# A second norm's inverse deviations inside an attention loop: Newton rounds on VectorE, or a first guess from ScalarE's tables

## What is computed

```
x = x + tanh(g1) * attention(layernorm(x), ctx, ctx)     16 heads of 8 channels
x = x + tanh(g2) * ffn(layernorm(x))
layernorm(x) = (x - mean) / sqrt(var + 1e-5)             over the 128 channels of a token
ffn(x) = mean over 2 shared experts + top 2 of 8 routed experts, 128 -> 512 -> 128, exact gelu
```

## Time and profile before

| | |
|---|---|
| median of 3 runs | 459.96 us (459.46 to 460.46) |
| the profiled execution | 462.34 us, its span 460.2 us |
| TensorE's mean granted clock | 0.968 |
| busy: DVE, PE | 387.0 us (84%), 386.7 us (84%) |
| busy: ACT, POOL | 339.0 us (74%), 310.6 us (67%) |

### The profile page before, as it was taken

One profiled execution on the slowest core, in us unless ns is written; L12 is line 12 of the kernel. 1 busy time (PEld: TensorE's weight loads), 2 busy tenths in 40 slices (PEclk: granted clock), 3 DMA queues, 4 the chain that ended last, 5 costly groups with the idle time before them and its releaser, 6 DMA issues.

```text
span 460.2 us, 14622 instructions
## 1 busy us (share of the span) xinstructions
PE 386.7 (84%) x5155; PEld 317.5 (69%) x5155; DVE 387.0 (84%) x950; ACT 339.0 (74%) x674; POOL 310.6 (67%) x431
## 2 busy tenths in 40 slices
PE   0566889996999899988779899998999999999910
PEld 0344767775888788776537676776899999999910
DVE  7797568977867977899788999887699999999986
ACT  0635678785888788878677987775788888888844
POOL 6252222898799999978777647775077777777740
PEclk9999899999999999999899999999899999999965
DMA  8967784354344244474121111112223333346129
GB/s 197 318 189 218 184 182 117 86 133 95 91 95 112 65 121 98 107 255 176 37 61 54 42 37 47 48 48 65 69 69 110 96 94 93 92 135 185 57 75 291
DMA packets 71685, 53.42 MB, mean 116 GB/s; under 512 B 7209, under 2 KB 63476, under 8 KB 71616
## 3 DMA queue, kind: packets, MB, share of 16 engines
q1 hardware_dynamic: 64896, 43.15, 35.5%
q0 software_dynamic: 4544, 8.44, 5.6%
q10 hardware_dynamic: 2176, 0.91, 0.8%
HBM read 29.51 MB, written 24.33 MB: 117 GB/s over the span
## 4 chain that ended last, share of the span: by engine, by line
POOL 30%; DVE 20%; issue 16%; PE 12%; DMA 11%; ACT 4%; SPq 3%; POOLq 0%; ACTq 0%; DVEq 0%
POOL yd L650 14%; DMA scr<-QKS 5%; POOL xs L628 3%; DVE HH L1532 3%; PE pAtt L1090 2%; POOL QKS L548 2%; DVE t_MX L1257 2%; POOL t_STG L558 2%; DMA t_K<-scr 2%; POOL t_W2l L562 2%; PE pS L1027 2%; DMA t_STG<-in_W 1%; POOL t_XF L572 1%; PE pE L1027 1%; PE pAtt L928 1%
## 5 line engine op out<-in xcount | busy, mean ns | idle before, releaser
L650 POOL DMA_INDIRECT yd<-Y,XR x78 | 87.4, 1121 | 38.4 <-issue 23.5
L1257 DVE TENSOR_REDUCE t_MX<-pS 128x4 f32<-128x512 f32 x128 | 86.7, 682 | 23.8 <-PE pS L889 21.6
L748 ACT ACTIVATE PT<-pE,t_mbias,t_scl 128x512 f32<-128x512 f32 x128 | 96.8, 787 | 3.7 <-PE pE L889 3.7
L628 POOL DMA_INDIRECT xs<-t_STG,t_pos x64 | 66.5, 1039 | 26.8 <-issue 13.4
L1562 DVE SCALAR_TENSOR_TENSOR HR<-GG,t_sc,HR 128x512 f16<-128x512 f32 x78 | 58.6, 751 | 2.8
L1144 PE MATMUL pAtt<-t_W2h,HR 128*128 x624 | 59.1, 219 | 0.7 <-DVE HR L1562 0.7
L889 PE MATMUL pS<-t_K,t_Q 128*128 128x128 f16 x512 | 50.9, 224 | 8.5 <-DVE t_MX L1257 5.4
L1144 PE MATMUL pAtt<-t_W2l,HR 128*128 x312 | 54.4, 219 | 0.0
L889 PE MATMUL pE<-t_Q,t_K 128*128 128x128 f16 x512 | 50.5, 222 | 2.6 <-DMA t_Q<-MPl 1.6
L828 ACT ACTIVATE GG<-pS,t_b1T,t_inv 128x256 f32<-128x256 f32 x78 | 39.8, 560 | 17.0 <-PE pS L1132 16.5
L1090 PE MATMUL pAtt<-t_W2h,HH 128*128 128x128 f16 x512 | 47.8, 222 | 4.3 <-DVE HH L1532 4.3
(11 more groups left out here) (280 smaller groups left out, 1041.8 us busy)
## 6 DMA issues: line engine op xcount, KB each, us to landing
xs<-t_padrow SPq DMA_DIRECT2D x10, 516.0 KB, 5.2
XR<-xs SPq DMA_DIRECT2D x39, 129.0 KB, 2.3
scr<-QKS SPq DMA_DIRECT2D x16, 256.0 KB, 2.4
t_Q<-scr SPq DMA_DIRECT2D x16, 256.0 KB
t_K<-scr SPq DMA_DIRECT2D x32, 128.0 KB
t_STG<-in_W SPq DMA_DIRECT2D x7, 512.0 KB, 6.8
YY<-yd SPq DMA_DIRECT2D x14, 256.0 KB, 4.6
t_X<-in_x SPq DMA_DIRECT2D x4, 512.0 KB, 7.3
```

The source lines that it names most:

```text
L628: g.indirect_dma_start(k.xs, bass.IndirectOffsetOnAxis(ap=pos[:, n:n + 1], axis=0), k.PAY[:, n, :], None).then_inc(h.di[q], 16)
L650: g.indirect_dma_start(k.yd, bass.IndirectOffsetOnAxis(ap=XR[u][:, q, D:ROW], axis=0), Y[u][:, q, :], None, bounds_check=2 * T - 1, oob_is ...
L748: act.activation(PT[:, m % NPT], pE[g % 2][:], ACT.Exp, bias=k.mbias[:, bt:bt + 1], scale=k.scl[:, bt:bt + 1]).then_inc(s.exp, 1)
L1257: v.tensor_reduce(out=MX[:, n // G % 2, n % G // 4, m % 2, m // 2::2], in_=pS[n % 2][:], axis=AX_X, op=ALU.max).then_inc(s.max, 1)
```

## The change

For the turns 8, 12, 16 and 18 the first guess comes from ACT: DVE adds epsilon in step 0 and raises a semaphore; ACT computes in its step 2 the logarithm, then `exp(-0.5 * ln(var + eps))` into `k.rstd`, and raises a second one; DVE waits for it in step 4, does one Newton round, two instructions of it in step 4 and the third in step 5, and `k.nmr` behind it. In turn 18 the generator is now called once per step as in the others. The pairs 14 and 15, after the loop, are computed as before. Three semaphores of the prologue are joined with others to make room for the three new ones; their instructions stay where they were.

```diff
+    SEEDED = sorted(t for t in RSTD if t < END)
...
+            def seed_deviations(t):
+                first, pairs = RSTD[t]
+                cols = slice(2 * first, 2 * (first + pairs))
+                act.wait_ge(l.var, SEEDED.index(t) + 1)
+                act.activation(tmpn[:, cols], tmpv[:, cols], ACT.Ln).then_inc(l.ln, 1)
+                act.wait_ge(l.ln, SEEDED.index(t) + 1)
+                act.activation(k.rstd[:, cols], tmpn[:, cols], ACT.Exp, scale=-0.5).then_inc(l.seed, 1)
...
+                    if g == 2 and t in SEEDED:
+                        seed_deviations(t)
...
+            def seeded_deviations(t):
+                first, pairs = RSTD[t]
+                cols = slice(2 * first, 2 * (first + pairs))
+                out, x, y = k.rstd[:, cols], tmpv[:, cols], tmpn[:, cols]
+                link(v.memset(tmpn[:, cols], 0.0))
+                link(v.tensor_scalar(x, k.mv[:, cols, 1], EPS, None, ALU.add))
+                settle(v, l.var)
+                for _ in range(4):
+                    yield
+                v.wait_ge(l.seed, SEEDED.index(t) + 1)
+                link(v.scalar_tensor_tensor(out=y, in0=out, scalar=-0.5, in1=out, op0=ALU.mult, op1=ALU.mult))
+                link(v.tensor_tensor(y, y, x, ALU.mult))
+                yield
+                link(v.scalar_tensor_tensor(out=out, in0=y, scalar=1.5, in1=out, op0=ALU.add, op1=ALU.mult))
+                v.scalar_tensor_tensor(out=k.nmr[:, cols], in0=k.mv[:, cols, 0], scalar=-1.0, in1=out, op0=ALU.mult, op1=ALU.mult).then_inc(l.rstd, 1)
+                yield
...
-                rstd = inverse_deviations(*RSTD[t]) if t in RSTD else iter(())
+                rstd = seeded_deviations(t) if t in RSTD else iter(())
...
                     next(rstd, None)
-                    if t == END - 2:
-                        next(rstd, None)
-                        next(rstd, None)
```

More of the change, by code:

```diff
@@ L312, in layer @@
     names = ("xn T XT qk qk32 hi lo ST S max mp nmT t2 exp pv ev tk at bt cp op x "
-             "st vp vev dv bias bvr any gb scl wm wk wb ws wh wl mb mr md ma qs st1 rs z zz sq zk")
+             "st vp vev dv bias bvr any gb scl wm wk wb ws wh wl mb mr qs st1 rs z sq zk")
     s = Parts(**{n: sem("a_" + n) for n in names.split()})
@@ L318, in layer @@
     N_W, N_RD, N_M = 16 * 3, 16 * 4, 16 * 2
-    l = Parts(**{n: sem("l_" + n) for n in "rstd xf pay T XT G gate idx route count slots".split()})
+    l = Parts(**{n: sem("l_" + n) for n in "rstd xf pay T XT G gate idx route count slots var ln seed".split()})
     h = Parts(**{n: sem("s_" + n) for n in "up gelu hi hia lo dn x exp wt".split()})
@@ L476, in body @@
                     if t == 2:
-                        sp.wait_ge(s.z, 1)
+                        sp.wait_ge(s.z, NB - 1)
                     wait(sp, s.ST, G * (t - NB + 1))
@@ L677, in values_in @@
                 if t == 2:
-                    act.wait_ge(s.z, 1)
+                    act.wait_ge(s.z, NB - 1)
                 wait(act, s.pv, G * (t - NB + 1))
@@ L729, in _ @@
                 act.activation(k.Q[u][:].rearrange("p a b -> p (a b)").bitcast(F32).rearrange("p (n d) -> p n d", d=P), eights,
-                               ACT.Copy, scale=0.0).then_inc(s.zz, 1)
-            act.wait_ge(s.zz, NB - 2)
+                               ACT.Copy, scale=0.0).then_inc(s.z, 1)
+            act.wait_ge(s.z, NB - 2)
             for u in range(2, NB):
@@ L876, in _ @@
             pe.transpose(pA[0][:, 1, 0:B], k.maskf[:], k.identf[0:B, 0:B]).then_inc(s.mr, 1)
-            pe.wait_ge(s.md, 1)
+            pe.wait_ge(s.mb, 2)
             pe.matmul(pA[1][:, 0, 0:5], k.ones[0:5, :], k.mxd[:], start=True, stop=True)
-            pe.matmul(pA[1][:, 1, 0:B], k.ones[:], k.maskT[:], start=True, stop=True).then_inc(s.ma, 1)
+            pe.matmul(pA[1][:, 1, 0:B], k.ones[:], k.maskT[:], start=True, stop=True).then_inc(s.mr, 1)
             pe.wait_ge(k.s_rest, k.rest_in)
@@ L1173, in _ @@
             link(v.tensor_reduce(out=k.mxc[:], in_=pA[0][0:5, 0, :], axis=AX_X, op=ALU.max))
-            v.tensor_scalar(k.mxd[:], k.identf[0:5, 0:5], k.mxc[:], None, ALU.mult).then_inc(s.md, 1)
-            v.wait_ge(s.ma, 1)
+            v.tensor_scalar(k.mxd[:], k.identf[0:5, 0:5], k.mxc[:], None, ALU.mult).then_inc(s.mb, 1)
+            v.wait_ge(s.mr, 2)
             v.tensor_scalar(k.anyb[:], pA[1][:, 1, 0:B], 1.0, None, ALU.min)
```

## The result

The changed kernel is slower: 465.11 us median of 12 runs (462.39 to 466.88), beside 460.44 us (458.12 to 463.92) for the kernel before on the same chip. The ratio is 1.0101, with an interval of 1.0077 to 1.0125. The forecast of 455.5 us was wrong in its sign, and the time lies outside the range.

What follows compares the result with a forecast made beforehand. POOL was taken to set the pace in turns 8 to 15, DVE in turns 16 to 18. Terms 1.3 + 1.0 + 1.9 + 0.3 = 4.5 us took the median from 459.96 to 455.5 us, range 454.0 to 457.2, chance 0.62.

Steps and rivals of the forecast that it cites:

- The step that failed: ACT's first logarithm, in turn 8, brings the only added table load, 1.28 us, covered by ACT's wait of 2.24 us.
- Rival 3: Each of four seeds loads tables twice, 3.1 us on ACT: 463 us; chance 0.10, shared with any other slower way.
- Turn 12's overrun: Two loads in turn 12 exceed ACT's holes; the loss is mostly taken back by POOL's slower pace. No size given.
- Turn 8: The second Newton round leaves DVE, so nmr and POOL's payload 0 come 1.3 us earlier; bounds 0 and 2.8.
- ACT's part: Two small activations per seeded turn, 0.5 us together, plus one load, covered by ACT's waits behind step 3.
- Turn 16: PE's plain scores no longer wait 0.81 us for DVE and come earlier: 1.0 us, lower bound 0.
- Turn 18 with the clock: DVE's block leaves, closing PE's 2.09 us hole: 1.9 us (0 to 2.1); PE's clock may not fall: 0.3 (0 to 0.7).
- Payload 12, the tie: Turn 18's later nmr makes payload 12 ready at 223.3 to 223.8, against PE's transpose_rows at 224.0.
- granted clock at 1.00 through 226: Sign of being right: with PE's turn 18 wait of 2.09 us gone, its clock stays full, instead of 0.50 from 224.
- The sum: Gains in turns 8, 16 and 18 plus the clock, 1.3 + 1.0 + 1.9 + 0.3 = 4.5 us, giving median 455.5.

Runs made afterwards that it cites:

- pair in turn 12: Kernel with one set, with a table load put back before the logarithm and one before the exponential in turn 12 alone: 455.88 us, ratio 0.9922.
- pair in turn 18: Kernel with one set, with the two table loads put back around the logarithm in turn 18 alone: 457.50 us, ratio 0.9935.
- one load in turn 8: Changed kernel with one load of the joint Exp and Ln set right before turn 8's logarithm, no other added load: 452.42 us, again 453.24 us.
- only turn 18 spread: Kernel before, with turn 18's three Newton rounds spread one stage per step over steps 0 to 5, no guess from ACT: 458.52 us, ratio 0.9971.
- kernel with one set: Changed kernel with the set holding both Exp and Ln loaded once at the layer's start, no loads in the seeded turns: 454.85 us, again 454.48 us.
- loads alone: Kernel before with only two table loads added at step 2 of turns 8, 12, 16 and 18: 462.0 us, ratio 1.0066.
- pair in turn 8: Kernel with one set, with the two table loads put back around the logarithm in turn 8 alone: 452.94 us, ratio 0.9854.
- pairs in 8 and 12: Kernel with one set, with the two table loads put back around the logarithm in both turns 8 and 12: 456.93 us, ratio 0.9926.

## Why the prediction was wrong, point by point

**The step that failed** is the sentence "Ln was not used before, so a table load comes with the first one: 1.28 us". It put the whole of the loads at one, from the silent assumption that one set stays loaded for both functions. Eight came. With the one load that the step assumed, the kernel gives 452.4 and 453.2 us, a gain; with eight, 465.1. What spoke for one load was a set that holds both functions. The Trainium skill, "ScalarE: Activation LUTs", section "Table sets: the hidden batching unit", says that a logarithm followed by an exponential takes one load, as there is a set with both. The runs agree with the half of it that such a set exists and serves both: the load at 106.19 above. They disagree with the count for code that names no set: there, each guess loaded twice.

**Rival 3 was the right one, at the wrong price.** It named two loads per seed, 3.1 us on ACT (2.93 measured), and gave 463 us at a chance of 0.10. Three parts of the price were too small. "Turn 12's overrun" was "mostly taken back by POOL's slower pace": it was not, the pair there costs 2.4 to 2.9 us up to the Gelu load. PE stood 2.54 us, and ACT's next queries and keys came late to POOL (with the pair in turn 12 alone):

```profile
161.81 0.61 POOL L547 CAST QKS<-QK 128x512 f16<-128x512 f32 x1 [1.56 <-ACT QK L667]
```

In the changed kernel POOL waited 1.19 us for payload 4 and 1.31 us there. The second part is turn 18, where PE was to come "about 0.7 later than before": with the pair in turn 18 alone, the Gelu load came 1.9 us later than before, counted from payload 8 (24.39 less 22.45). And the clock was left out: over 104 to 232 us the granted clock of the changed kernel was 0.95 on average, against 1.00 and 0.99 in the two executions with one load in turn 8. How much time that is was not separated.

**Turn 8** (forecast 1.3 us). POOL's wait before payload 0 fell to 1.54 us in the changed kernel, and to 0.64 and 0.33 in the two executions with one load in turn 8. But that wait is a poor measure: it was 2.81 us in the kernel before and 1.54 in the one with only turn 18 spread, whose turn 8 is the same code. There the second round, from which the 1.3 was read, took 0.7 us instead of 1.33: two of its instructions took 0.17 and 0.25 us where the profile of before had 0.54 each. So the 1.3 was read from one execution and does not repeat. By these waits the term lies between 0.9 and 2.5 and stays no sharper.

**ACT's part, other than the loads**, was right. Two activations of 0.21 us, and a cover of ACT's wait in turn 8 that shrinks "to under 0.6": 0.57 and 0.17 with one load there. That 0.57 is so close to 2.24 less (1.28 + 0.5) is luck, as the same wait without a load in the turn was 1.03 and 1.56.

**Turn 16** (forecast 1.0). Without the added loads payload 7 to payload 8 takes 8.08 us instead of 9.48: 1.4 us.

**Turn 18 with the clock** (forecast 1.9 + 0.3). Payload 8 to the Gelu load falls from 22.45 to 20.29 us: 2.2 us. The hole of 2.09 us is gone and the clock stays at 1.00 up to the Gelu load. The experiment with the block spread shows that the reason given, the block's place, carries 1.7 of the 2.2 up to that mark, but 1.0 of 2.2 up to PE's first matmul of the shared experts.

**Payload 12, the tie.** With one set, PE waits 0.74 us for it in turn 19; with the eight loads, POOL has it at 224.98 after a wait of 4.94 us. The 0.74 us alone are the small loss that a tie allows. But the forecast's sign "granted clock at 1.00 through 226" held only in part, and right behind this wait. Of the four executions with one load, two keep 1.00 there and two do not. PE's wait, then two windows of the first execution of the kernel with one set, then the same two windows of its second (columns as above):

```profile
220.21 0.40 PE L980 MATMUL pMix<-t_ident,t_STG 128*128 128x128 f16 x4 [0.74 <-POOL t_STG L578]
```

```profile
220.00:222.00 2.00, 1.51 (x11) 1.06 (x12) 1.13 (x5) 1.58 (x5) 1.69 (x5) 1.00 0.00 0
222.00:224.00 2.00, 2.00 (x21) 1.39 (x20) 0.88 (x4) 1.03 (x3) 1.71 (x3) 1.00 0.00 0
```

```profile
220.00:222.00 2.00, 1.72 (x10) 0.93 (x8) 0.76 (x4) 1.18 (x5) 1.85 (x5) 0.70 0.00 0
222.00:224.00 2.00, 2.00 (x12) 1.16 (x12) 0.83 (x3) 0.27 (x1) 1.40 (x3) 0.50 0.00 0
```

**The sum.** Turn 8's term aside, the rows give 1.4 + 2.2 = 3.6 us, where the forecast had 3.2. With one load in turn 8, the times give 1.5% to 1.7%, about 7 us (by the intervals 5 to 9.5); with it at the layer's start 1.2% to 1.3%, about 5.6. With 0.9 to 2.5 for turn 8 the rows explain 4.5 to 6.1; whether anything is left over, and where, stays open. The forecast's range was narrow at this end for one reason that can be named: it counted turn 8 with at most 1.6, while its own bound for that term was 2.8.

## What to carry to other kernels

Before a second function is put on ScalarE, count its table loads from the changed program or fix the set by hand: a set that holds both functions helps only if it is the one loaded. Place the load where the engine already waits: there the traces show no price. Read a term from more than one execution where the same code can be profiled twice. And price an addition to an idle engine with the holes that remain after the change: eight loads cost 3 us in the kernel before, and 10 us in the one with the shorter VectorE list.

## What the runs showed of the hardware that was not expected

A table load took 1283 ns each time, for the logarithm, the exponential and Gelu alike, and the activation behind it started 0.01 us after its end (107.48 + 1.28, then 108.77). The drain of some 1.38 us that the Trainium skill adds to a switch ("ScalarE: Activation LUTs", section "What ACT_TABLE_LOAD costs") is not seen in any of these rows.

The clock fell at the end of a hole of PE or just behind it, and stayed low for some us in which PE was busy. Behind standing 2.54 us (pair in turn 12) two windows of 2 us have 0.53 and 0.62, which is 1.9 and 1.5 us at the lower level. In the changed kernel's turn 18, with PE standing 3.14 us, four windows have 0.69, 0.50, 0.50 and 0.60, which is 6.8 us. So a wait for a table load may cost more than the load.

The length of the hole alone does not say whether the clock falls. With the loads alone in the kernel before, PE stood 2.20 us in turn 12 (up to 155.86) and the clock stayed at 1.00 from 156 to 160 us. With the seed, PE's wait of 0.74 to 0.76 us in turn 19 was followed by a fall in three executions (the second ones of both one-load kernels, and the pair in turn 8) and by none in four (their first ones, the pair in turn 12, the pairs in 8 and 12). What decides it stays open.

This fall is where executions of one and the same kernel part. The two of the kernel with one set agreed within 0.1 us up to the Gelu load (104.45 and 104.56 from payload 0), but from there to the second half of the scatter they took 48.09 and 49.69 us. In all seven executions just named that stretch is 48.1 us without the fall and 49.7 with it. The second execution was at the lower level for 3.4 us (windows of 0.70, 0.50 and 0.95), which at the full clock is 1.7 us of work. A step's gain is therefore better read in the stretch where it arises than in the total of a single execution.
